# First group of heads with value products over a tile's whole width; the first layer's values from rows of the key products and transposes

## What is computed

```python
x = x + attn_a(layernorm(x))   # 16 query heads, 4 key/value heads of 16 features, biases, rotary angles, causal
x = x + ffn(layernorm(x))      # hidden 2048, 4-bit weights unpacked with scales, tanh gelu, gate * up, down
x = x + attn_b(layernorm(x))   # 16 heads of 16 features, no biases, no rotary angles, causal
x = x + ffn(layernorm(x))      # the same weights again
```

## Time and profile before

| | |
|---|---|
| median of 3 runs | 1857.38 us (1852.73 to 1858.48) |
| profiled execution | 1860.16 us, span of its trace 1858.3 us |
| TensorE busy | 1752.0 us (94%) |
| VectorE, ScalarE, GpSimd busy | 1152.0, 951.9, 544.1 us |
| mean granted TensorE clock | 0.952 of full |

### The profile page before, as it was taken

One profiled execution on the slowest core, in us unless ns is written; L12 is line 12 of the kernel. 1 busy time (PEld: TensorE's weight loads), 2 busy tenths in 40 slices (PEclk: granted clock), 3 DMA queues, 4 the chain that ended last, 5 costly groups with the idle time before them and its releaser, 6 DMA issues. The chain is left out here.

```text
span 1858.3 us, 33821 instructions
## 1 busy us (share of the span) xinstructions
PE 1752.0 (94%) x13822; PEld 1124.6 (61%) x13822; DVE 1152.0 (62%) x1664; ACT 951.9 (51%) x1879; POOL 544.1 (29%) x454
## 2 busy tenths in 40 slices
PE   7799999999999989999988899999999998999998
PEld 5554444555444568888876544445544456788887
DVE  5445777677886547554555567776777663754554
ACT  2123457666777634444422245777667774444443
POOL 4211356668777612333320010000000000233332
PEclk8785789999999999999998889999999999999999
DMA  5111313405201042000003215060150101400000
GB/s 133 44 35 26 45 49 65 81 23 94 51 33 68 36 172 117 1 1 1 0 0 119 84 25 69 1 84 11 19 75 2 36 2 76 197 12 1 13 11 11
DMA packets 50487, 89.30 MB, mean 48 GB/s; under 512 B 20920, under 2 KB 35000, under 8 KB 48072
## 3 DMA queue, kind: packets, MB, share of 16 engines
q1 hardware_dynamic: 45560, 70.99, 16.2%
q0 software_dynamic: 4256, 15.78, 2.7%
q10 hardware_dynamic: 528, 0.52, 0.1%
HBM read 58.17 MB, written 28.84 MB: 47 GB/s over the span
## 5 line engine op out<-in xcount | busy, mean ns | idle before, releaser
L1142 DVE TENSOR_REDUCE chunk_max<-ring 128x2 f32<-128x1024 f32 (+3 forms) x640 | 674.0, 1064 | 268.4 <-PE ring L882 164.8
L1038 ACT ACTIVATE probs<-ps_s 128x512 f32<-128x512 f32 (+3 forms) x1280 | 624.2, 534 | 359.3 <-PE ps_s L913 187.1
L1443 POOL TENSOR_TENSOR inter_lo<-inter,inter_hi 128x512 fp32r<-128x512 f32 x128 | 165.4, 1292 | 893.5 <-ACT inter_hi L1391 893.5
L882 PE MATMUL ring<-xnt 63*128 63x512 f32 (+3 forms) x640 | 249.4, 488 | 25.6 <-DVE chunk_max L1142 8.1
L882 PE MATMUL ring<-region_rounded 63*128 63x512 f32 (+3 forms) x640 | 254.9, 447 | 5.8 <-DVE chunk_max L1142 4.5
L908 PE MATMUL ps_s<-xnt 64*128 64x512 f32 (+3 forms) x640 | 254.3, 448 | 4.9 <-ACT probs L1038 4.2
L908 PE MATMUL ps_s<-region_rounded 64*128 64x512 f32 (+3 forms) x640 | 229.4, 441 | 4.3 <-ACT probs L1038 4.2
L908 PEld LDWEIGHTS ps_s<-xnt 64*128 64x128 f32 x640 | 113.7, 196 | 140.3 <-ACT probs L1038 107.0
L925 PE MATMUL ps_o<-probs,unit_plain 128*32 128x256 f32 (+1 forms) x2304 | 188.4, 401 | 0.0
L1372 ACT ACTIVATE gelu_a<-ps_g 128x512 f32<-128x512 f32 x128 | 76.5, 598 | 216.9 <-PE ps_u L87 216.9
L1416 DVE SCALAR_TENSOR_TENSOR gelu_a<-gelu_a,ps_g 128x512 f32<-128x512 f32 x128 | 87.9, 686 | 154.7 <-ACT gelu_a L1372 154.3
(11 more groups left out here) (206 smaller groups left out, 2934.5 us busy)
## 6 DMA issues: line engine op xcount, KB each, us to landing
w_mlp<-w_scr SPq DMA_DIRECT2D x32, 768.0 KB, 14.5
w_scr<-region_rounded POOLq DMA_DIRECT2D x16, 768.0 KB, 3.8
region_rounded<-q_scr SPq DMA_DIRECT2D x24, 256.0 KB, 7.9
q_scr<-region_rounded SPq DMA_DIRECT2D x16, 192.0 KB, 2.3
xnt<-q_scr SPq DMA_DIRECT2D x12, 256.0 KB, 9.0
xnt<-w_scr SPq DMA_DIRECT2D x4, 768.0 KB, 5.6
q_scr<-region_rounded SPq DMA_DIRECT2D x8, 384.0 KB, 3.5
k_scr<-region_rounded SPq DMA_DIRECT2D x8, 384.0 KB, 3.5
```

The source lines that it names most:

```text
L882: op = pe.matmul(out[:, h, 0:w], qt[g][plain[h], p, q0:q0 + P], kt[g][plain[h], p % NKP, c * TW:c * TW + w], start=True, stop=c < t)
L1038: act.activation(pr[n % NPR][:, h, w0:TW], src[:, 0:TW - w0], ACT.Exp, scale=SCALE).then_inc(s_e, 1)
L1142: dve.tensor_reduce(mp[rank[y[1:3]] % 2][:, qb, 2 * p:2 * p + 2, c], ring[n % 2][:, :, 0:w], AX.X, ALU.max).then_inc(s_rd, 1)
L1443: pool.tensor_tensor(il[n % NI][:, :], ti[n % 2][:, :], ih[n % NI][:, :].bitcast(F32), ALU.subtract).then_inc(s_il, 1)
```

## The change

Two things are changed.

1. In the first layer the product `PJ t, 2` with the plain weights takes 128 weight columns instead of 64: rows 64 to 127 of its output are the values with features on partitions. ScalarE copies those 64 rows to a new tile `vt` (64 x 512). `VJ t` is then 4 transposes of 64 x 128 (K = 64 rows, 64 columns each) instead of 24 matmuls, and stands behind `PJ t + 1, 0` in the list, that of tile 3 behind `RL 3, 0`. VectorE's second rotary step of f = 2 waits for the copy. `VJ t - 1` must be out of `vt` before the next copy. The wait of GpSimd's value copy (`s_v0`) moves from the first `M` of a tile to the tile's first `PV`. GpSimd follows the list too. The four `M` pairs of tile 1's opening stand behind its last projection.
2. In both layers `PV` of the first group is one product over all columns, 4 matmuls of up to 512 columns before head 0, where there were two of 4 matmuls of 256.

```diff
 def projection(t, shared):
-    return [("PJ", t, f) for f in range(3 if shared else 2)] + [("VJ", t)]
+    return [("PJ", t, f) for f in range(3)] if shared else [("PJ", t, 0), ("PJ", t, 1), ("VJ", t)]
+def values(t, shared):
+    return [("VJ", t)] if shared else []
...
             if k == 0:
+                plan.extend(values(t - 1, extra) if t else [])
                 plan.extend(beside)
-            if k == len(items) - 3:
+            if k == (1 if extra else 0):
                 plan.extend([("TU", t + 1), *after_turn])
...
-    opening(1, [0, 0, 2, 2], [], [("N", 3)])
-    opening(2, [2, 2, 2, 2] if extra else [2, 3, 3])
+    opening(1, [0, 0, 4] if extra else [0, 2, 2], [], [("N", 3)])
+    opening(2, [2, 2, 4] if extra else [2, 3, 3])
...
-                    if at < 2 or h == (0 if at == BT - 1 else 2):
-                        plan.append(("PV",) + done + (1 if at >= 2 else h // 2,))
+                    if done[0] == 0:
+                        if h == 0:
+                            plan.append(("PV",) + done + (WHOLE,))
+                    elif at < 2 or h == (0 if at == BT - 1 else 2):
+                        plan.append(("PV",) + done + (WHOLE if at >= 2 else h // 2,))
...
+                        if rope and a == 0:
+                            count = P
...
+                    if rope:
+                        pe.wait_ge(s_vt, t + 1)
                     out = slot(y)
-                    at = 2 * P + 64 if rope else 4 * P
                     for b in range(BT):
-                        for k in range(KC):
+                        if rope:
+                            op = pe.transpose(v_block(out, b), vt[64:P, b * P:(b + 1) * P], per["ident"][64:P, 64:P])
+                        for k in range(0 if rope else KC):
...
                             pe.wait_ge(s_e, laid_out(t))
-                            pe.wait_ge(s_v0, t + 1)
...
-                    c = slice(max(width(t, kb), TW // 2 * part), TW // 2 * (part + 1))
+                        if g == 0:
+                            pe.wait_ge(s_v0, t + 1)
+                    c = slice(max(width(t, kb), TW // 2 if part == 1 else 0), TW if part else TW // 2)
...
+                        if y[2] == 2:
+                            act.wait_ge(s_rf, ringed[y] + 1)
+                            if y[1]:
+                                act.wait_ge(s_rf, ringed[("VJ", y[1] - 1)] + 1)
+                            act.activation(vt[64:P, :], ring[ringed[y] % 2][64:P, 0, :], ACT.Copy).then_inc(s_vt, 1)
...
+                if f == 2:
+                    dve.wait_ge(s_vt, t + 1)
```

More of the change, by code:

```diff
@@ L302 @@
 LATE = 2
+WHOLE = 2
 PRE = 2
@@ L386, in attention_plan @@
     for k, y in enumerate(items):
-        later[k * BT * GH // len(items)] = (laid[k] if k < len(laid) else []) + [y]
+        later[k * BT * GH // len(items)] = (laid[k] if k < len(laid) else []) + [y] + (values(NT - 2, extra) if k == 0 else [])
     for k, x in enumerate(relayout(NT - 1, extra)):
-        later[BT * GH + 2 + 4 * k] = x
+        later[BT * GH + 2 + 4 * k] = x + (values(NT - 1, extra) if k == 0 else [])
     turned = {30: ("WL", 1), 36: ("W", 1), 42: ("WL", 2), 50: ("W", 2), 56: ("WL", 3), 64: ("W", 3)} if extra else {}
@@ L441, in attention_plan @@
             if half or done[2] - BT * done[1] < 2:
-                plan.append(("PV",) + done + (half,))
+                plan.append(("PV",) + done + (half if done[2] - BT * done[1] < 2 else WHOLE,))
         plan += [o for o, _ in turns[:2]]
@@ L564, in attention_block @@
             ra, rb = ([early.take((TW,)) for _ in range(2)] for _ in range(2))
+            vt = early.take((TW,))
         mp = [t_.sb(f"chunk_max{i}", [P, BT, GH, NT]) for i in range(2)]
@@ L592, in attention_block @@
             s_bs, s_ra = t_.sem("s_bias_sign"), t_.sem("s_rope_a")
+            s_vt = t_.sem("s_v_turned")
         NF_T, N_OUT = 3 if rope else 2, 16 * 2
@@ L607, in attention_block @@
         scored, rows = places([y for y in plan if y[0] in scored_kinds]), places([y for y in plan if y[0] == "R"])
-        pvs = places([y[:4] for y in plan if y[0] == "PV" and y[4] == 1])
+        pvs = places([y[:4] for y in plan if y[0] == "PV" and y[4]])
         turned = places([y for y in plan if y[0] in ("W", "TU", "AT", "MT")])
@@ L925, in _ @@
                         last = pe.matmul(ps_o[32 * h:32 * h + VC, c], v, pr[n % NPR][:, h, c],
-                                         start=kb == 0 and part == 0, stop=kb == BT * (t + 1) - 1)
+                                         start=kb == 0 and part != 1, stop=kb == BT * (t + 1) - 1)
                     if part:
@@ L1038, in _ @@
                     act.activation(pr[n % NPR][:, h, w0:TW], src[:, 0:TW - w0], ACT.Exp, scale=SCALE).then_inc(s_e, 1)
-                elif y[0] == "PV" and y[4] == 1 and y[3] == BT * (y[2] + 1) - 1:
+                elif y[0] == "PV" and y[4] and y[3] == BT * (y[2] + 1) - 1:
                     act.wait_ge(s_pv, pvs[y[:4]] + 1)
```

33 lines of the change are left out of this document (17 added, 16 removed).

## The result

The changed kernel takes 1848.32 us in the median of 9 runs (1839.21 to 1854.13), beside 1856.88 us of the kernel before on the same chip (9 runs). The ratio is 0.9946, 95% interval 0.9927 to 0.9965: 8.6 us faster, where 28 were forecast. It lies just outside the range of 1809 to 1847, on its slow side.

A forecast was written before the change was run, and what follows sets the result against it. TensorE was taken to set the time inside the first group, a TensorE-VectorE chain in the opening. Terms 15 + 4 + 6 + 3 = 28 us off 1860.16 gave 1832, a median of 1829, range 1809 to 1847.

The forecast's parts named there:

- term 1: First layer's opening: value matmuls leave the path and products run at a higher clock, 15 us less (10 to 17).
- term 2: First layer's first query tile: shorter VJ 3 and faster filling matmuls behind it, 4 us less (2.5 to 5.5).
- Term 3: First group, both layers: merging 64 pairs of value products saves fixed costs, 6 us less (nothing to 9.0).
- term 4: First group's low clock in tiles 1 and 2 of the first layer: 3 us less.
- rival D: Merged key blocks: the long value product lets VectorE run dry, making the kernel slower, 1871 us; chance 0.04.
- Rival E: Whole kernel: losses of about 0.4 us cancel the opening's gain, no effect to be seen, 1855 us; chance 0.04.
- Rival B: Opening: the chain through VectorE, GpSimd and ScalarE lets only 6 us come off instead of 15, 1838 us; chance 0.12.
- Rival C: First group's value products: the fixed cost is not saved, gain 0 to 1.3 us, 1834 us; chance 0.1.
- rival A: First layer's tiles 1 and 2: the low clock ends early, a further 18 us less, 1811 us; chance 0.2.
- At nothing: Costed at zero: wider key-product weights, four ScalarE copies (2.4 us at most), later value copies and stores, moved value wait.
- the signs named: Expected in the trace: earlier opening products, first score step and o_t copy, 1.0 us value products, shorter later second-layer stages.
- signs of being wrong: Opening above 75 us, TensorE's reduction waits up over 6 us, or stages outside opening and two first groups moving.

The follow-up runs named there:

- e2: The kernel before with only the first group's whole-width value products, values still by 24 matmuls: 1850.13 us, ratio 0.9959.
- e1: The changed kernel with the first group's value products in two halves again, new values kept: 1862.70 us against 1857.99, ratio 1.0025.
- e17: The kernel before with only the places of the first group's two value halves changed, to before heads 1 and 3: 1807.39 us, ratio 0.9738.
- e18: The changed kernel with the first group's value products in two halves, before head 1 and before head 3: 1809.49 us, ratio 0.9753.
- e5: The changed kernel plus 104 filling matmuls that compute nothing in idle places of the first layer's opening: 1835.20 us, ratio 0.9858.
- e4: The changed kernel with two half value products directly behind each other before head 0 instead of one whole: 1846.01 us, ratio 0.9940.
- e9: The changed kernel with the first group's whole value product before head 3 instead of head 0: 1814.34 us, ratio 0.9801.
- e11: The kernel before, unchanged, run once more for a second trace: 1860.25 us.
- e12: The changed kernel with value products in halves again and new values kept, run again for a second trace: 1865.09 us.

## Why the prediction was wrong

**The step that failed is term 1, "the opening: 15 us less", and with it term 2, "4 us less": the 19 us of the first part of the change.** e2 shows that the second part alone gives 7.9 of the 8.6 us. The first part adds 0.7 us to it, within the intervals; alone it costs 4.7 (e1), and beside the halves before heads 1 and 3 it is worth nothing (e17, e18). Two things stand in its place. The opening itself became 6.5 to 7.5 us shorter instead of 15, because the products left in it ran at the low clock. And what did come was lost again: the second layer's attention takes 3 to 10 us more in every pair of traces, with a lower clock. The prediction took for granted that time saved in the opening is saved at the end.

**Term 3, "the whole value products: 6 us less", failed in its mechanism, and that its size fits is luck.** With the 3 us of term 4 the second part was forecast at 9, and e2 measured 7.9, but as a gain by the clock in the earlier tiles (57.6 to 47.1 us in tile 1 of the first layer, 45.3 to 40.8 in the second) less a loss by place in the later ones. The term's price of one product was right: 0.99 us against the forecast 1.0. It was multiplied by 64 as if TensorE were the bound in every key block, and the discount of a third was a guess; "a gain of nothing" as the lower bound left out a loss. The stage is a loop of three engines with two slots and three banks, and a key block with the whole product before head 0 takes 0.43 us longer in tile 3. At a full clock that costs 5.3 us in the second layer's tile 3 and 2 us in its tile 2.

That is rival D's mechanism at the price D named as its break-even (0.44 us), but only in the later tiles. I gave D 0.04 with the argument that two slots hold 2.2 us of reductions at the start of a product. The trace shows VectorE idle for 1.17 us there, and when the product began at 1164.77 VectorE had 0.65 us of work left (1163.06 + 2.36 = 1165.42). The other slot was half full: of a pair of maximum matmuls that share a slot one stood ahead of the product and one behind it, so the slot could not be reduced until the product was over. Rival E named losses of that kind against the opening's gain; it comes nearest to what the stages show, but its 1855 us, no effect to be seen, is not what was measured.

**Rival B's number came, and its mechanism did not.** B said that the chain through VectorE, GpSimd and ScalarE would let only 6 us off the opening. The opening gained about that much, but e5 takes it to 63.4 us with the same chain in it.

**The rule that the Trainium skill gave**, a fixed cost of 2.5 ns for a warm matmul (TensorE: Matmul & The Clock Gate, "Wait — 56ns, not 53.3ns?"), is in accord with e4: two halves directly behind each other cost 1.01 us against 0.99 for one product. The 0.13 us of the earlier trace rows is paid once where value products stand among other work, and not for each product. My term took it for a cost of the product, and against the rule I wrote that the rows speak for 0.13. Rival C said that it would not be saved; merging a pair did save 0.15 us (0.99 for 2 x 0.57), of which 0.13 come from standing side by side alone.

**Term 1, 15 us: 7.5 came, 6.5 of them by the change.** The matmuls went out as described. `PJ 1, 1` starts 5.2 us earlier than before and `PJ 2, 0` 8.5 us (54.88 for 63.33). 2.2 us of both were there already at the first transposes of tile 1 (22.95 for 25.18), ahead of anything that was changed: 0.9 by an earlier start and 1.3 by the first product's clock. That leaves 3.0 and 6.2, where 3.2 and 8.0 had been forecast. Then it stops. "The clock fell while `VJ 2` ran, so with it gone I expect this one product at full clock" failed: `PJ 3, 0` took 5.4 us instead of 2.8, and `PJ 2, 0` stayed low too. It was also misread. From 89.94 to 92.73 us, where `VJ 2` stood, the granted clock was 1.00; it fell in the maximum matmuls behind it (0.69 from 92.73 to 93.97). `PJ 2, 1`, which stood at the full clock before, is low now for most of its matmuls, and from `PJ 2, 0` to the maximum matmuls at 74.01 us (80.39 before) 2.1 of the 8.5 us are lost again. e5 shows that the clock was what was missing. My lower bound of 10 let the clock give nothing; that it could take was not in it.

**Term 2, 4 us: 0.75 came** (37.67 for 38.42). The clock of that stage is 0.86 for 0.91, and the 24 filling matmuls took 4.45 us, not the 2.78 hoped for.

**Term 4 and rival A.** Of the low stretch of tile 1 I wrote "Nothing in the change must end it", and took 3 us. It ended: 11.7 us less in tile 1 and 5.6 in tile 2 (the latter net of the loss by place), which is nearly all that rival A named. So A's condition came true, at a chance of 0.2, and the time was still 37 us above A's. e1 and e2 show that the value products' order did this. It hid how far the other terms fell short: with tile 1 as long as in e1 (13.9 us more) the changed kernel would by this estimate have come out slower than before.

**At nothing.** The wider key product costs nothing (0.23 us apart at full clock). The four copies were not seen as a wait. "TensorE is busy 92% to 99% of each stage" was read too high: in the first layer's tiles 0 and 2 it is 90% and 91%.

Of the signs named, `PJ 1, 0` near 32 (29.9) and the 1.0 us held. The first score step near 86 (92.8), the first `o_t` copy near 121 (130.5), `PJ 3, 0` in 2.8 us and the later stages all shorter did not. Of the three signs of being wrong all showed: the opening stayed above 75 us, by 0.75; TensorE's waits for the reductions in the three stages of the earlier trace rows went from 9.0 to 16.4 us; and stages outside the opening and the two first groups moved, such as the second layer's tile 1 of the third group, 24.8 for 23.4 us.

## What to carry to other kernels

Before pricing a saving on the busiest engine, read one period of its loop by the timelines of all engines and ask where in the period it waits; a long step belongs there, and the same step elsewhere costs more than it saves (3.27 against 2.65 us for the same instructions). Before pricing removed work in a stretch with a low clock, ask what keeps the clock up once it is gone: here filling the idle places was worth more than the removal. And a gain shown by one stage should be checked against a kernel that differs in that part alone and by its whole time: here 6.5 us in the opening were worth nothing at the end.

## What the runs showed of the hardware

A low clock lasted very differently long at the same place of the program, and being busy did not end it. Slices of 4 us in tile 1 of the kernel before, where all slices from 147 to 203 us stand at 0.50; columns as in the stages:

```profile
159.00:163.00 4.00, 4.00 (x30) 1.88 (x29) 2.15 (x2) 1.58 (x3) 2.08 (x4) 0.50 1.17 164
...
187.00:191.00 4.00, 4.00 (x29) 1.86 (x28) 1.36 (x2) 1.14 (x3) 0.00 (x0) 0.50 0.18 39
```

And in the changed kernel:

```profile
142.00:146.00 4.00, 4.00 (x21) 1.64 (x14) 1.68 (x2) 0.83 (x2) 4.00 (x2) 0.50 0.00 0
146.00:150.00 4.00, 4.00 (x20) 1.33 (x17) 2.69 (x3) 1.79 (x3) 4.00 (x7) 0.50 0.59 94
150.00:154.00 4.00, 3.79 (x26) 2.00 (x18) 1.90 (x2) 1.69 (x3) 0.66 (x1) 0.65 1.07 132
```

TensorE is busy for nearly every moment in both (3.55 us or more of each 4 in the low stretch before). Before, the low clock stays for some 60 us; in the changed kernel it is over after about 14. In e9, with the product before head 3, this tile has no low clock at all. In the first group the granted clock repeats from run to run of the same kernel (e11 and e12), so it follows the order of the program there; no row tells what ends it.
